# Turned score maxima copied by ScalarE instead of VectorE, and the slots of the maxima packed and respaced

## The reference, cut to what matters

```
scores = jnp.einsum('bqhd,bkd->bhqk', q, k) * scale
scores = jnp.where(causal[None, None], scores + alibi[None], NEG_INF)
probs = jax.nn.softmax(scores, axis=-1)
attn = jnp.einsum('bhqk,bkd->bqhd', probs, v).reshape(B, S, H)
```

## Time and profile before

| what | us |
|---|---|
| median of 3 executions | 702.86 (701.89 to 704.84) |
| the profiled execution, its own time | 700.96 |
| its span, first to last instruction | 699.2 |
| steps 5 to 9 and steps 10, 12 to 15, each | 30.82 and 27.77 |
| TensorE busy, VectorE busy | 669.7, 557.4 |

### The profile page before, as it was taken

One profiled execution on the slowest core, in us unless ns is written; L12 is line 12 of the kernel. 1 busy time (PEld: TensorE's weight loads), 2 busy tenths in 40 slices (PEclk: granted clock), 3 DMA queues, 4 the chain that ended last, 5 costly groups with the idle time before them and its releaser, 6 DMA issues.

```text
span 699.2 us, 13261 instructions
## 1 busy us (share of the span) xinstructions
PE 669.7 (96%) x4304; PEld 305.5 (44%) x4304; DVE 557.4 (80%) x1801; ACT 358.6 (51%) x511; POOL 216.9 (31%) x366
## 2 busy tenths in 40 slices
PE   3889999999999999999999999999999999999997
PEld 2434344544344444444443343433433455555553
DVE  5899889887989889898988989899881365666565
ACT  2324647567556676666666666767667411111111
POOL 0035424233332515243352231422432412222220
PEclk9999999999999999999999999999999999999999
DMA  8578108080411443080144744225200189700001
GB/s 253 130 145 137 64 2 136 30 147 28 166 54 51 60 89 108 11 131 34 41 63 94 102 81 77 49 49 94 48 18 33 52 130 170 162 30 30 31 30 60
DMA packets 42951, 56.32 MB, mean 81 GB/s; under 512 B 6648, under 2 KB 26232, under 8 KB 42752
## 3 DMA queue, kind: packets, MB, share of 16 engines
q1 hardware_dynamic: 40296, 51.27, 37.3%
q10 hardware_dynamic: 2592, 4.26, 1.8%
HBM read 35.72 MB, written 19.79 MB: 79 GB/s over the span
## 4 chain that ended last, share of the span: by engine, by line
PE 83%; DVE 10%; DMA 3%; ACT 2%; issue 1%; SPq 1%; POOL 0%; DVEq 0%; ACTq 0%; POOLq 0%
PE psum L780 20%; PE psum L732 18%; PE psum L762 13%; PE psum L808 8%; PE psum L830 7%; PE psum L678 7%; PE psum L759 5%; DVE psum L1145 3%; PE psum L825 2%; PE psum L840 2%; ACT work L965 2%; DMA x_sb<-in_x 1%; DVE negm L1150 1%; PE psum L817 1%; DMA arena<-q_dram 1%
## 5 line engine op out<-in xcount | busy, mean ns | idle before, releaser
L965 ACT ACTIVATE work<-psum 128x1024 f32<-128x1024 f32 (+1 forms) x320 | 289.0, 943 | 127.6 <-PE psum L762 108.5
L1145 DVE CUSTOM_DVE_ANT_0 psum<-psum,future 128x384 f32<-128x384 f32 (+3 forms) x512 | 237.7, 514 | 12.6 <-PE psum L732 10.4
L732 PE MATMUL psum<-k_op,arena 106*128 106x512 bf16 (+3 forms) x768 | 212.4, 328 | 9.6 <-DVE negm L1145 4.3
L1150 DVE TENSOR_REDUCE negm<-psum 128x1 f32<-128x512 f32 x256 | 168.6, 687 | 15.3 <-PE psum L732 10.9
L1318 POOL TENSOR_SCALAR_AFFINE_SELECT work<-work 128x512 f32<-128x512 f32 x128 | 81.2, 634 | 296.2 <-ACT work L965 296.2
L780 PE MATMUL psum<-work,v_op 128*32 128x512 f32 (+3 forms) x1536 | 163.5, 498 | 0.5 <-POOL work L1318 0.4
L762 PE MATMUL psum<-arena,k_op 109*128 109x512 bf16 (+3 forms) x640 | 157.3, 316 | 1.9 <-ACT work L965 0.8
L732 PEld LDWEIGHTS psum<-k_op,arena 106*128 106x128 bf16 x768 | 69.0, 97 | 128.5 <-DVE negm L1145 40.7
L678 PE MATMUL psum<-arena,wqkv_sb 128*128 128x256 f32 (+3 forms) x240 | 84.6, 453 | 1.1 <-ACT arena L887 1.1
L759 PE MATMUL psum<-arena,k_op 116*128 116x128 bf16 x512 | 84.3, 221 | 0.9 <-ACT work L965 0.9
L762 PEld LDWEIGHTS psum<-arena,k_op 109*128 109x128 bf16 x640 | 59.6, 98 | 44.5 <-ACT work L965 15.7
(11 more groups left out here) (86 smaller groups left out, 454.8 us busy)
## 6 DMA issues: line engine op xcount, KB each, us to landing
arena<-q_dram SPq DMA_DIRECT2D x96, 128.0 KB, 5.5
o_dram<-o_sb SPq DMA_DIRECT2D x32, 256.0 KB
q_dram<-arena SPq DMA_DIRECT2D x16, 384.0 KB, 4.4
arena<-o_dram SPq DMA_DIRECT2D x32, 128.0 KB, 4.6
arena<-rcp_dram SPq DMA_DIRECT2D x32, 128.0 KB, 4.9
out<-wqkv_sb ACTq DMA_DIRECT2D x16, 256.0 KB, 2.0
x_sb<-in_x SPq DMA_DIRECT2D x3, 1024.0 KB, 10.0
work<-in_x SPq DMA_DIRECT2D x3, 1024.0 KB, 18.8
```

The costliest lines, as they stand in the source:

```text
L732: last = nc.tensor.matmul(bank[:, a * width:(a + 1) * width], q_op[0:ROW_MAX, bass.ds(col, P)], k_op[0:ROW_MAX, b, k0:k0 + width], start=T ...
L965: nc.scalar.activation(probs[:, n % 4, heads * hp:heads * (hp + 1), 0:w], src, ACT.Exp).then_inc(exp_done, 1)
L1145: last = nc.vector.tensor_tensor_reduce(keys, keys, future[:, CH - width:CH], -1.0, 3e38, ALU.add, ALU.min, negm[:, late, 0, j * QT + t:j ...
L1150: nc.vector.tensor_reduce(dst, psum[:, bank, 0:len(js) * width].rearrange("p (a k) -> p a k", a=len(js)), AX_X, ALU.max, negate=True).then ...
```

## The change

It does six things. The t = 0 maxima of a head share a slot with its t = 2 maxima, so that all diagonal slots have 512 columns and a step has 36 slots. The two turns are no slots any more: they stand behind a slot of TensorE's list (`turn_behind`), the late turn behind the third slot of the next step, and use a bank of the same ring. ScalarE copies the turned maxima (`copy_maxima`), in the place of its list where side work is evicted. VectorE's late diagonal reductions take the full maximum as their start value, a column of `negm` in place of a number, and the join is gone; they wait until the full slot's result is written. Slots are spread over 1.02 instead of 0.95 of the step. Where TensorE waits for the keys 512 to 1023 of a batch, it now does so at the first late diagonal slot.

```diff
-TURN_AFTER = 3
+TURN_AFTER = (3, 3)
...
-SLOTS_BY = 0.95
+SLOTS_BY = 1.02
...
-    out = []
-    for t in range(QT):
-        if late:
-            out += [("full", late, t, (j,)) for j in range(UH)]
-        per = 2 if t < 2 else 1
-        out += [("diag", late, t, tuple(range(j, j + per))) for j in range(0, UH, per)]
-    return out
+    full = [[("full", late, ((j, t),)) for j in range(UH)] for t in range(QT)]
+    pairs = [("diag", late, ((j, 1), (j + 1, 1))) for j in range(0, UH, 2)]
+    uneven = [("diag", late, ((j, 2), (j, 0))) for j in range(UH)]
+    wide = [("diag", late, ((j, 3),)) for j in range(UH)]
+    if not late:
+        return uneven + pairs + wide
+    return full[0] + full[1] + pairs + full[2] + uneven + full[3] + wide
 EARLY_SLOTS = len(max_slots(0))
 SLOTS = max_slots(0) + max_slots(1)
-TURN = [EARLY_SLOTS + TURN_AFTER, len(SLOTS) + 1]
-SLOTS.insert(TURN[0], ("turn", 0, None, None))
-SLOTS.insert(TURN[1], ("turn", 1, None, None))
 NSL = len(SLOTS)
+FIRST_LATE_DIAG = min(r for r, (kind, late, _) in enumerate(SLOTS) if kind == "diag" and late)
...
+def turn_behind(k, put):
+    if put == EARLY_SLOTS + TURN_AFTER[0]:
+        return [("turn", 2 * k, None)]
+    if put == TURN_AFTER[1] and k:
+        return [("turn", 2 * k - 1, None)]
+    return []
...
-        while k < NK and put < NSL - 1 and slot_due(k, put) * total <= done:
+        while k < NK and put < NSL and slot_due(k, put) * total <= done:
             out.append(("slot", k, put))
             put += 1
+            out += turn_behind(k, put)
         out.append(piece)
-    return out + [("slot", k, r) for r in range(put, NSL if k < NK else 0)]
+    for r in range(put, NSL if k < NK else 0):
+        out.append(("slot", k, r))
+        out += turn_behind(k, r + 1)
+    return ([("turn", NU - 1, None)] if k == NK else []) + out
...
-                kind, late, t, js = SLOTS[r]
+                kind, late, parts = SLOTS[r]
                 bank, before = SLOT_AT[k, r]
                 bank_free(before)
                 bank = psum[:, bank]
-                if kind == "turn":
-                    if late:
-                        pe.wait_ge(max_late, k + 1)
-                    else:
-                        pe.wait_ge(slot_free, NSL * k + EARLY_SLOTS)
-                    nc.tensor.transpose(bank[0:UH * QT, 0:P], negm[:, late, 0, :], ident[:]).then_inc(slot_full, 1)
-                    return
...
-                if k % NB == 0 and r in (0, EARLY_SLOTS):
+                if k % NB == 0 and r in (0, FIRST_LATE_DIAG):
                     pe.wait_ge(k_ready, 2 * b + (1 if r == 0 else 2))
...
-                width = P * (t + 1) if kind == "diag" else CH
-                k0 = CH * late if kind == "diag" else 0
-                for a, j in enumerate(js):
+                k0, at = CH * late if kind == "diag" else 0, 0
+                for j, t in parts:
+                    width = P * (t + 1) if kind == "diag" else CH
                     col = unit_col(2 * k + late, j, None) + t * P
-                    last = nc.tensor.matmul(bank[:, a * width:(a + 1) * width], q_op[0:ROW_MAX, bass.ds(col, P)],
+                    last = nc.tensor.matmul(bank[:, at:at + width], q_op[0:ROW_MAX, bass.ds(col, P)],
                                             k_op[0:ROW_MAX, b, k0:k0 + width],
                                             start=True, stop=True)
+                    at += width
                 last.then_inc(slot_full, 1)
+            def turn_maxima(u):
+                bank, before = TURN_BANK[u]
+                bank_free(before)
+                pe.wait_ge(slot_free, NSL * (u // 2) + (NSL if u % 2 else EARLY_SLOTS))
+                nc.tensor.transpose(psum[0:UH * QT, bank, 0:P], negm[:, u % 2, 0, :], ident[:]).then_inc(turn_full, 1)
...
+            def copy_maxima(u):
+                act.wait_ge(turn_full, u + 1)
+                if u >= 2:
+                    act.wait_ge(m_split, u - 1)
+                nc.scalar.copy(m_t[:, u % 2], psum[0:UH * QT, TURN_BANK[u][0], 0:P]).then_inc(turn_done, 1)
+            def evict(what, n):
+                if what == "side":
+                    side(n)
+                else:
+                    copy_maxima(n)
...
-            def step(k, i=None, some=range(NSL)):
+            def step(k, some=range(NSL)):
                 for r in some:
-                    kind, late, t, js = SLOTS[r]
+                    kind, late, parts = SLOTS[r]
                     idx = NSL * k + r
                     bank = SLOT_AT[k, r][0]
-                    if kind == "turn":
-                        u = 2 * k + late
+                    if k and r in (0, EARLY_SLOTS):
+                        dve.wait_ge(turn_full, 2 * k - 1 + late)
+                    dve.wait_ge(slot_full, idx + 1)
+                    if kind == "diag":
                         if late:
-                            dve.wait_ge(slot_free, at_loop(idx, i, 2 * NSL))
-                            nc.vector.tensor_tensor(negm[:, 1, 0, :], negm[:, 1, 0, :], negm[:, 1, 1, :], ALU.min
-                                                    ).then_inc(max_late, 1)
-                        dve.wait_ge(slot_full, at_loop(idx + 1, i, 2 * NSL))
-                        if u >= 2:
-                            dve.wait_ge(m_split, at_loop(u - 1, i, 4))
-                        nc.vector.tensor_copy(m_t[:, u % 2], psum[0:UH * QT, bank, 0:P]).then_inc(slot_free, 1)
-                        continue
-                    dve.wait_ge(slot_full, at_loop(idx + 1, i, 2 * NSL))
-                    width = P * (t + 1) if kind == "diag" else CH
-                    where = 1 if kind == "full" else 0
-                    if kind == "diag":
-                        if i is not None:
-                            dve.nop(nofuse=True)
-                        for a, j in enumerate(js):
-                            keys = psum[:, bank, a * width:(a + 1) * width]
-                            last = nc.vector.tensor_tensor_reduce(keys, keys, future[:, CH - width:CH], -1.0, 3e38, ALU.add, ALU.min,
-                                                                  negm[:, late, 0, j * QT + t:j * QT + t + 1])
+                            dve.wait_ge(slot_free, NSL * k + max(SLOTS.index(("full", 1, (part,))) for part in parts) + 1)
+                        at = 0
+                        for j, t in parts:
+                            width, to = P * (t + 1), j * QT + t
+                            keys = psum[:, bank, at:at + width]
+                            last = nc.vector.tensor_tensor_reduce(keys, keys, future[:, CH - width:CH], -1.0,
+                                                                  negm[:, 1, 1, to:to + 1] if late else 3e38, ALU.add, ALU.min,
+                                                                  negm[:, late, 0, to:to + 1])
+                            at += width
                         last.then_inc(slot_free, 1)
                         continue
-                    dst = negm[:, late, where, :].rearrange("p (j t) -> p j t", t=QT)[:, js[0]:js[-1] + 1, t]
-                    nc.vector.tensor_reduce(dst, psum[:, bank, 0:len(js) * width].rearrange("p (a k) -> p a k", a=len(js)),
-                                            AX_X, ALU.max, negate=True).then_inc(slot_free, 1)
+                    (j, t), = parts
+                    nc.vector.tensor_reduce(negm[:, late, 1, j * QT + t:j * QT + t + 1], psum[:, bank], AX_X, ALU.max, negate=True
+                                            ).then_inc(slot_free, 1)
...
-                pool.wait_ge(slot_free, at_loop(NSL * (u // 2) + TURN[u % 2] + 1, i, 2 * NSL))
+                pool.wait_ge(turn_done, u + 1)
```

45 lines of the change are left out of this document (28 added, 17 removed).

## The result

The changed kernel takes 704.25 us (median of 22 executions, 702.47 to 705.25) where the one before takes 702.67 (22 executions beside it): ratio 1.0025, 95% interval 1.0015 to 1.0034. That is slower by 1.6 us: the interval leaves out 1, but it is within the 0.5% that the prediction counts as no change. The forecast was 7.4 us less, with a range of 689 to 702, and 704.25 lies above it. The profiled execution's span is 702.9 us.

What follows compares the result with a forecast made beforehand. TensorE and VectorE were taken as close to matched. Gains of 1.9 (late steps), 0.9 (step 11), 2.5 (steps 5 to 9) and 3.2 (steps 1 to 4), less 1.1, gave 7.4 us: median 695.5 us, range 689 to 702.

Steps and rivals of the forecast that it cites:

- Step 0: First step: VectorE's copy and join go out, column operands come in; no gain or loss counted.
- The marks: Signs of right: no VectorE copies, late steps 27.3 to 27.5, late reductions 0.05 to 0.1 longer, transpose 0.3 late.
- Late steps, 0.37 each: Five late steps: each loses about 0.4 us to waits instead of 0.77, 1.9 us gained in all.
- 0.2 us more buffer: Packing: 40 slots become 36 longer ones, so three banks hold 0.2 us more VectorE work; counted in the waits.
- Steps 5 to 9, 1.1 becomes 0.6: Steps with a projection: TensorE's lost time falls from 1.1 to 0.6 us each, 2.5 us gained in all.
- The pool: TensorE's lost time that could be won: 20.2 us in all, 1.1 a step in steps 5 to 9.
- Steps 1 to 4, 0.8 each: Steps where VectorE sets the pace in stretches and is 0.9 us shorter: 0.8 us gained each, 3.2 in all.
- Step 11, 0.9: Step with the reciprocals: they start 1.35 us earlier, but the turn waits for the slot behind; 0.9 us gained.
- Column operand, 0.07: Late reductions reading their start value from a column: 0.07 us each, 16 in a step, 1.1 us of VectorE.
- The charge of 1.1 for the late turn's chain: Late scores or GpSimd's zeroing coming late behind the moved turn, in steps 1 and 11: 1.1 us lost in all.
- The rivals: Against a 3.5 to 12 us gain (0.62): operand or second wait eats it (0.22), slower late chain (0.11), more won (0.05).
- Rival C: Steps 5 to 15: late scores wait behind copy, split, store and load; 5 us slower, 708 us; chance 0.11.

Runs made afterwards that it cites:

- e10: The kernel before, with step 0's four normalisations behind slots 18 to 21 instead of 14 to 17: 705.72 us, ratio 1.0043.
- e2: The changed kernel with step 0's normalisations behind slots 10 to 13 and key-split pieces behind slots 1 to 7: 699.61 us, ratio 0.9965.
- e9: e2 with normalisations behind slots 9 to 12 and, per step, another spread, slots run ahead and late-turn place: 704.11 us, single execution.
- e3: The changed kernel with VectorE, not ScalarE, copying the turned maxima, at the same place of TensorE's order: 707.22 us, ratio 1.0074.
- e7: The changed kernel with the slots unpacked as before, 40 slots: 708.0 us, ratio 1.0073.
- e4: The changed kernel with late diagonal reductions starting from the constant 3e38 instead of the column: 702.6 us, ratio 0.9997.
- e8: The kernel before with slots spread over 1.02 of the step instead of 0.95: 709.34 us, ratio 1.0094.
- e6: e2 with slots spread over 0.95 of the step instead of 1.02: 702.98 us, ratio 1.0.

## Why the prediction was wrong, by its own steps

- **Step 0, "copy and join out, operands in, nothing."** Measured +3.47, the largest change of any single step, and second in the sum behind steps 5 to 9. The instructions' count and kinds were right; what I had not asked is where VectorE's side work, pinned to slot numbers, would stand against GpSimd's work. e10 makes the like loss in the kernel before (about 3.2), e2 and e9 take it away. The Trainium skill has the rule, which I should have weighed: "SBUF — State Buffer", section "Who interferes with whom", says that VectorE and GpSimd share a pair of SBUF ports under an exclusive lock: a VectorE instruction with two SBUF inputs contends with a GpSimd instruction that reads SBUF, a copy, cast or `tensor_scalar` can contend when it runs in a two-port mode, and one with at most one SBUF input outside those modes doesn't. The traces agree: 1.34 for 0.15 (two SBUF inputs) and 1.47 for 0.53 us (`tensor_scalar`), while full reductions from PSUM beside the same splits keep their 0.68. That the normalisations run in a two-port mode is not shown by any row.
- **The marks.** VectorE's copies and its idle time at the turn are gone, the transpose is 0.35 late behind its bank, ScalarE's copy starts 2.1 us behind the step's first slot (269.46 for 267.39 in step 7), late steps are 27.34: all as forecast, and all of them in steps that I had looked at. One mark was missed: late reductions are 0.02 to 0.045 longer than early ones, not 0.05 to 0.1.
- **Late steps, 0.37 each.** Right in size, 0.43, and in its pieces: the bank of slot 0 costs 0.35 (0.3 forecast) and slot banks about 0.1 (0.1). The reason given was half right: the copies and the join out of VectorE are worth 0.2 to 0.5 (e3, copies alone), packing 0.56 (e7), for which I had set nothing but 0.2 us more buffer. The pieces add to more than the 0.43 measured, so each is worth that much only in the order that it was tested in.
- **Steps 5 to 9, 1.1 becomes 0.6.** This term failed most, by 4.5 us of the sum, and wrong in sign: +0.40 each. The pool was mis-sized: by the same subtraction before loses 0.31 at the turn's bank, 0.18 for exponentials and 0.10 for slots, 0.6 and not 1.1, and only 0.1 of that was to be had. And a bank wait is not the only thing that slots prevent: fewer, longer slots, respaced, changed what stands between score pieces, and 0.61 is lost there to exponentials. Neither ScalarE's copies (e3) nor VectorE's load (e4) cause it. Which of the order's parts does is settled only partly. Lost for exponentials in step 7 are 0.18 us before, 0.43 in the old order spread over 1.02 (e8), 0.49 with the turn moved and the slots unpacked (e7) and 0.61 in the changed kernel; but 0.95 in the new order leaves them at 0.61 (e6), so the spread alone does not explain them, and what does stays open.
- **Steps 1 to 4, 0.8 each.** Half: 1.66 together, and unevenly (-1.78, +1.43, -0.42, -0.89). VectorE's busy time over these steps did not fall, 116.6 us for 116.7; only its idle time did, from 17.5 to about 16. In step 2 it is busy 30.23 for 28.82, and 0.8 of that is key pieces from SBUF to SBUF that last longer. The rest of step 2's loss was not taken apart.
- **Step 11, 0.9.** Measured 0.75, by the mechanism named: the turn waits for the slot behind the reciprocal (391.19 below).
- **Column operand, 0.07.** Measured 0.023 to 0.045, and it mattered less than that: 0.6 us of VectorE in a step reach TensorE as 0.08.
- **The charge of 1.1 for the late turn's chain.** Hardly paid: in no step from 5 on do the changed kernel's late scores wait for their load, and in step 1 the first value piece loses 0.30 to GpSimd's zeroing. Step 15 lost 0.49 by something unforeseen: its late turn stands first in step 16, with no work ahead of it, and TensorE waits 0.52 for VectorE's last slot and 0.55 more for ScalarE's copy ahead of the first output projection.

Timelines of the changed kernel for steps 11 and 15: VectorE and TensorE at the start of step 11, TensorE at the end of step 15.

```profile
388.62 1.75 DVE L1188 RECIPROCAL sums<-sums 128x256 f32<-128x256 f32 x1
```

```profile
391.19 0.28 PE L758 MATMUL psum<-ident,negm 128*16 128x128 f32 x1 [1.51 <-DVE negm L1176]
...
526.96 0.27 PE L758 MATMUL psum<-ident,negm 128*16 128x128 f32 x1 [0.45 <-DVE negm L1176]
527.62 1.10 PE L834 MATMUL psum<-wo_sb,wqkv_sb 128*128 128x512 f32 x2 [0.39 <-ACT m_t L956]
```

The sum went wrong by 9.2 us against the steps: step 0 by 3.5, steps 5 to 9 by 4.5, steps 1 to 4 by 1.5, the late steps (15 with them) by 0.6, step 11 by 0.15, less the charge of 1.1. Steps 5 to 9 and step 0 alone turn 7.4 us of gain into none. The rivals missed it too, since all of them were about VectorE's load or the late chain: none about where its side work lies, and none about waits for exponentials. Rival C has the right sign by the wrong way, since its chain did not come late.
